# Attention with a layer norm and a gated feed-forward: the value products of the second pair of rows on stacked keys

## What is computed

```python
xn = layernorm(x)                                  # x: (8, 1024, 256)
q = (xn @ Wq + bq) in 8 heads of 128, + pe         # keys and values are shared by the heads
k, v = split(xn @ Wkv + bkv);  k = k + pe          # 128 columns each
probs = softmax(causal(q @ k.T / sqrt(128)))
attn = (probs @ v) @ Wo
out = x + attn + sigmoid(mr(xn) @ W_r.T) * (relu(mk(xn) @ W_k.T)**2 @ W_v.T)
```

## Time and profile before

| | |
|---|---|
| median of 3 runs | 1500.66 us (1500.39 to 1500.99) |
| the profiled execution, its own time | 1500.61 us |
| span of its instructions | 1498.9 us (1.7 us lie around it) |
| TensorE busy | 1477.3 us, 99% |
| VectorE, GpSimd, ScalarE busy | 1254.5 us (84%), 1158.2 us (77%), 1068.7 us (71%) |
| DMA | 171.73 MB, mean 115 GB/s |

### The profile page before, as it was taken

The page is one execution under the profiler, slowest core; times in us unless marked ns, Lnnn a source line. Parts: engine busy times, 40 slices in busy tenths (PEclk is TensorE's granted clock), DMA queues, the critical chain, the costliest instruction groups (busy, mean ns, idle before and its releaser), DMA issues.

```text
span 1498.9 us, 36110 instructions
## 1 busy us (share of the span) xinstructions
PE 1477.3 (99%) x11668; PEld 1443.2 (96%) x11668; DVE 1254.5 (84%) x3408; ACT 1068.7 (71%) x2547; POOL 1158.2 (77%) x1541
## 2 busy tenths in 40 slices
PE   7999999999999999999999999999999999999998
PEld 6999999999999999999999999999999999999998
DVE  6989868898688986889868898788977899778885
ACT  5777677776777767777677776777667776777774
POOL 5677877778777887777877778777787787877785
PEclk8999999999999999999999999999999999999999
DMA  4134532346214462144612346124551345502463
GB/s 130 33 107 131 181 95 56 109 132 192 75 52 125 133 186 75 50 123 135 192 60 67 117 143 188 46 75 119 162 173 34 85 125 157 173 25 85 127 182 128
DMA packets 225801, 171.73 MB, mean 115 GB/s; under 512 B 43600, under 2 KB 220880, under 8 KB 225616
## 3 DMA queue, kind: packets, MB, share of 16 engines
q1 hardware_dynamic: 224768, 169.03, 37.8%
q10 hardware_dynamic: 848, 0.40, 0.1%
HBM read 84.94 MB, written 81.26 MB: 111 GB/s over the span
## 4 chain that ended last, share of the span: by engine, by line
PE 85%; DVE 9%; issue 3%; POOL 1%; ACT 0%; DMA 0%; DVEq 0%; POOLq 0%; ACTq 0%
PE pS L1040 29%; PE pO L1181 22%; PE pG L1040 14%; PE pG L1127 9%; PE pT L1143 8%; DVE X L1019 2%; PE pS L1127 1%; DVE mix L860 1%; DVE Y L923 1%; DVE pt L943 1%; DVE xn L808 1%; POOL xt L509 1%; DVE ot L998 1%; DVE qtmp L849 1%; DVE kt L831 0%
## 5 line engine op out<-in xcount | busy, mean ns | idle before, releaser
L1040 PE MATMUL pS<-kt,qt 128*128 128x288 f32 (+41 forms) x2304 | 459.8, 329 | 1.7 <-POOL qt L521 1.1
L764 ACT ACTIVATE X<-X,bias 128x16 f32<-128x16 f32 (+56 forms) x512 | 375.9, 734 | 118.4 <-DVE bias L1019 117.7
L571 POOL TENSOR_SCALAR X<-X,rec 128x16 f32<-128x16 f32 (+56 forms) x512 | 379.2, 741 | 75.0 <-DVE rec L913 64.1
L1040 PEld LDWEIGHTS pS<-kt,qt 128*128 128x128 f32 x2304 | 366.1, 189 | 14.1 <-issue 2.0
L546 POOL TENSOR_TENSOR pt<-pt 128x896 fp32r<-128x896 f32 (+4 forms) x192 | 340.1, 1774 | 34.8 <-ACT pt L686 33.7
L1181 PE MATMUL pO<-pt,v 128*128 128x256 f32 x2192 | 307.1, 284 | 1.1 <-DVE ot L998 0.9
L1019 DVE CUSTOM_DVE_ANT_1 X<-pS,mask 128x528 f32<-128x528 f32 (+31 forms) x256 | 245.5, 959 | 37.8 <-PE pS L1040 33.4
L1181 PEld LDWEIGHTS pO<-pt,v 128*128 128x128 f32 x2192 | 272.0, 189 | 2.3 <-DVE ot L998 1.8
L757 ACT CAST ot<-pO 128x256 fp32r<-128x256 f32 x256 | 96.0, 375 | 203.0 <-PE pO L1181 116.9
L943 DVE TENSOR_TENSOR pt<-pt,pT 128x512 fp32r<-128x512 f32 (+3 forms) x424 | 197.3, 484 | 34.1 <-ACT pt L692 30.9
L692 ACT CAST pt<-pT 128x512 fp32r<-128x512 f32 (+3 forms) x432 | 182.0, 448 | 43.7 <-PE pT L1143 42.2
(11 more groups left out here) (123 smaller groups left out, 2259.3 us busy)
## 6 DMA issues: line engine op xcount, KB each, us to landing
park_dram<-Y SPq DMA_DIRECT2D x48, 448.0 KB, 3.2
pt<-park_dram SPq DMA_DIRECT2D x192, 112.0 KB, 3.0
park_dram<-Y SPq DMA_DIRECT2D x32, 512.0 KB, 2.9
pt<-park_dram SPq DMA_DIRECT2D x128, 128.0 KB, 2.9
park_dram<-Y SPq DMA_DIRECT2D x32, 384.0 KB, 2.9
pt<-park_dram SPq DMA_DIRECT2D x128, 96.0 KB, 2.4
park_dram<-Y SPq DMA_DIRECT2D x32, 320.0 KB, 2.7
pt<-park_dram SPq DMA_DIRECT2D x128, 80.0 KB, 2.2
```

What stands on the lines that cost most here:

```text
L571: nc.gpsimd.tensor_scalar(x_row(s, 0, w), x_row(s, 0, w), rec[:, j:j + 1], sign(s), ALU.mult, ALU.mult).then_inc(normed, 1)
L764: nc.scalar.activation(x_row(s, 0, w), x_row(s, 0, w), ACT.Exp, bias=bias[:, j:j + 1], scale=-1.0, accum_out=total[:, j:j + 1]).then_inc(e ...
L1040: last = nc.tensor.matmul(out, a[i], m[j], start=start and k == 0, stop=stop and k == n - 1)
```

## The change

The second pair of rows 1 to 7 (steps with `s % 8` of 2 and 3) has at most 64 keys in its diagonal block. Those keys are now written twice: on keys 0 to 63 and again on 64 to 127 of the block. Two tiles of values go with it: `vd` holds `v[0]` of the 64 keys on partitions 0 to 63 and `v[1]` on 64 to 127, `vz` holds `vn` on 0 to 63 and zeros below. `vd` x `pt[0]` and `vz` x `pt[1]` then take the place of the three products of that block. The other blocks of the pair keep three. Beside it `qtmp` has three slots in place of four, and some entries of the tables move. Of those in `F_LAG`, `H_LAG`, `L_LAG` and `W_LAG` only one concerns a step that is turned: the even steps of row 4 are fetched one iteration earlier.

```diff
-F_LAG = ((6, 1), (4, -2), (5, 4), (4, 3), (5, 3), (4, 1), (5, 5), (5, 2))
+F_LAG = ((5, 1), (4, -2), (5, 4), (4, 4), (4, 3), (4, 2), (5, 5), (5, 2))
-QTMP = 4
+QTMP = 3
-AT = {'stats': (-15, -8, -12, -7), 'apply': (-4, 0, 0, 0), 'inv': (-10, -5, -6, -3), 'mixr_prev': (0, 0, 0, 0), 'mixr_dve': (0, 0, 1, 0), 'mixr_out': (2, 1, 4, 1), 'ka_out': (4, 5, 9, 7), 'mixk_prev': (4, 7, 8, 4), 'mixk_dve': (6, 10, 8, 7), 'mixk_out': (9, 14, 11, 12)}
+AT = {'stats': (-15, -8, -14, -7), 'apply': (-4, -1, 0, 0), 'inv': (-12, -5, -6, -7), 'mixr_prev': (0, 0, 1, 0), 'mixr_dve': (0, 0, 1, 0), 'mixr_out': (2, 1, 4, 1), 'ka_out': (3, 4, 8, 7), 'mixk_prev': (4, 7, 8, 4), 'mixk_dve': (6, 10, 8, 9), 'mixk_out': (9, 14, 11, 12)}
...
+def doubled(s):
+
+    return s >= H and s % H // 2 == 1
...
+            def stack_two(b, c):
+
+                n = b * NC + c
+                sp.wait_ge(v_ready, n + 1)
+                if n:
+                    sp.wait_ge(pv_done, (n * TPC - 1) * PAIRS + 2)
+                tiles = slice(c * TPC, (c + 1) * TPC)
+                sp.wait_ge(v_neg, n + 1)
+                for to, part in ((vd[0:64, :, :], v[0]), (vd[64:P, :, :], v[1]), (vz[0:64, :, :], vn)):
+                    sp.dma_start(to.bitcast(F), part[0:64, tiles, :].bitcast(F)).then_inc(vd_loaded, 16)
+
             for b, it in turns():
                 if it < STEPS and it % PER == (2 if it >= PER else 11):
                     stack(b, it // PER)
+                if it < STEPS and it % PER == (6 if it >= PER else 13):
+                    stack_two(b, it // PER)
...
+                    elif doubled(s):
+                        own = (s % H + 1) * SUB
+                        last = x_row(s, s // H * P, (s // H + 1) * P).rearrange("p (i n) -> p i n", i=2)
+                        if own < 4 * SUB:
+                            nc.gpsimd.memset(last[:, :, own:4 * SUB], 0.0).then_inc(normed, 1)
+                        nc.gpsimd.tensor_scalar(last[:, 1, 0:own], last[:, 0, 0:own], rec[:, j:j + 1], sign(s),
+                                                ALU.mult, ALU.mult).then_inc(normed, 1)
+                        pool.wait_ge(normed, b * N_BODY + N_FIRST[s + 1] - 1)
...
+            nc.vector.memset(vz[64:P, :, :].bitcast(F), 0.0).then_inc(vs_zero, 1)
...
-                    work = [(k, i, j) for i, j in ((0, 0), (1, 0), (0, 1)) for k in range(plain)]
+                    work = ([(v[0][:, k, :], 0, k) for k in range(whole)] + [(v[1][:, k, :], 0, k) for k in range(whole)]
+                            + [(vd[:, tile, :], 0, k) for k in range(whole, plain)]
+                            + [(vn[:, k, :], 1, k) for k in range(whole)] + [(vz[:, tile, :], 1, k) for k in range(whole, plain)])
...
+                            if doubled(part):
+                                pe.wait_ge(vd_loaded, 48 * (b * NC + part // PER + 1))
```

More of the change, by code:

```diff
@@ L22 @@
 V_LAG = 3
[L23 to L26 removed]
+F_LAG = ((5, 1), (4, -2), (5, 4), (4, 4), (4, 3), (4, 2), (5, 5), (5, 2))
+H_LAG = ((6, 6), (6, 7), (7, 7), (7, 6), (7, 6), (7, 6), (7, 7), (7, 9))
+L_LAG = ((5, 4), (5, 5), (7, 6), (8, 12), (7, 9), (8, 13), (8, 7), (7, 7))
+W_LAG = ((9, 8), (11, 7), (8, 5), (6, 4), (7, 3), (7, 7), (8, 8), (8, 12))
 MODE = ('0000', '0000', '0111', '0111', '1111', '1111', '1313', '1111')
@@ L74, in packed, with used @@
     return s >= H and s % H < 2
+def doubled(s):
+    return s >= H and s % H // 2 == 1
+def used(s):
+    return 2 * SUB if packed(s) else 4 * SUB if doubled(s) else P
 def sign(s):
@@ L105, in scaled_by_act @@
 def scaled_by_act(s):
-    return s in SCALED and not packed(s)
+    return s in SCALED and not packed(s) and not doubled(s)
 def width(s):
@@ L178 @@
 T_BODY = T_FIRST[STEPS]
-N_FIRST = [sum((SUB * 2 if packed(r) else P) > (r % H + 1) * SUB for r in range(s))
-           + sum((not scaled_by_act(r)) + packed(r) for r in range(s)) for s in range(STEPS + 1)]
+N_FIRST = [sum(used(r) > (r % H + 1) * SUB for r in range(s))
+           + sum((not scaled_by_act(r)) + packed(r) + doubled(r) for r in range(s)) for s in range(STEPS + 1)]
 N_BODY = N_FIRST[STEPS]
@@ L222, in build @@
         vs = sb("vs", [P, TPC, D], R)
+        vd = sb("vd", [P, TPC, D], R)
+        vz = sb("vz", [P, TPC, D], R)
         vn = sb("vn", [P, NT, D], R)
@@ L292, in build @@
         vs_loaded = sem("vs_loaded")
+        vd_loaded = sem("vd_loaded")
         within_lo = sem("within_lo")
@@ L651, in v_out @@
                     act.wait_ge(vs_loaded, 48 * (chunk_no(b, c) - NC + 1))
+                    act.wait_ge(vd_loaded, 48 * (chunk_no(b, c) - NC + 1))
                 tiles = slice((c % NC) * TPC, (c % NC + 1) * TPC)
@@ L1156, in turn @@
                     plain = nk - packed(2 * pair)
+                    whole = nk - packed(2 * pair) - doubled(2 * pair)
+                    tile = part // H % TPC
                     summed = pO[:, 0:2 * P].rearrange("p (t a c) -> p t a c", t=2, a=4)
-                    work = [(k, i, j) for i, j in ((0, 0), (1, 0), (0, 1)) for k in range(plain)]
+                    work = ([(v[0][:, k, :], 0, k) for k in range(whole)] + [(v[1][:, k, :], 0, k) for k in range(whole)]
+                            + [(vd[:, tile, :], 0, k) for k in range(whole, plain)]
+                            + [(vn[:, k, :], 1, k) for k in range(whole)] + [(vz[:, tile, :], 1, k) for k in range(whole, plain)])
                     for n in range(len(work)) if part % 2 else ():
-                        k, i, j = work[n]
+                        standing, j, k = work[n]
                         if n == 0:
@@ L1171, in turn @@
                                     pe.wait_ge(t_hi, b * T_BODY + T_FIRST[s + 1])
-                        if n == 2 * plain:
+                        if n == len(work) - plain:
                             for s in (2 * pair + 1, 2 * pair):
@@ L1180, in turn @@
                                     pe.wait_ge(t_lo, b * T_BODY + T_FIRST[s + 1])
-                        last = nc.tensor.matmul(summed, (vn if j else v[i])[:, k, :],
-                                                pt_of(j, b, part)[:, :, :, k, :],
-                                                start=n == 0, stop=n == 3 * nk - 1)
+                        last = nc.tensor.matmul(summed, standing, pt_of(j, b, part)[:, :, :, k, :],
+                                                start=n == 0, stop=n == len(work) - 1 and not packed(part))
                     if part % 2:
@@ L1233, in _ @@
             pe.wait_ge(w_lo["wk"], 1)
-            pe.wait_ge(vs_zero, 1)
+            pe.wait_ge(vs_zero, 2)
             for b, it in turns():
```

2 lines of the change are left out of this document (1 added, 1 removed).

## The result

The changed kernel takes 1504.55 us (median of 8 runs, 1503.67 to 1505.42) against 1500.38 us (8 runs, 1499.62 to 1500.99): a ratio of 1.0026, 95% interval 1.0017 to 1.0035. The forecast was 1494.2 us with a range up to 1498.0.

The account below looks back on a forecast made before the run. TensorE was taken to bound the steady part; 1500.61 us less 6.5 us for 56 removed products, all else at nothing, gave 1494.1, forecast as 1494.2 us. The range was 1491.0 to 1498.0 us.

Parts of the forecast that it names:

- The bound: Steady part of the kernel: TensorE, busy 99% of the span, sets the time as long as the other engines keep up.
- The products: TensorE, second pairs of rows 1 to 7: 56 products less at 0.116 us each, 6.5 us off (6.3 to 7.8).
- third rival: Removed products only lengthen TensorE's wait for the same late tile, so nothing is gained: 1500.6 us, chance 0.05.
- Nothing for all of it: Query-sum slots, moved entries and the clear of vz cost zero, within -4.9 to +4 us.
- Slots and tables: Section on three query-sum slots and moved table entries: spare time suffices, no instruction is added or removed, cost nothing.
- the rival in which the tables cure TensorE's present waits: Moved entries also remove TensorE's existing waits: up to 4.9 us more gain, 1489.5 us, chance 0.08.
- I cost GpSimd's addition at nothing: GpSimd's added scalings, 43 us of its time (up to 80), stay hidden and add zero to the kernel's time.
- The margins: Room before TensorE needs late tiles: 2.35 us at the mask, 5.4 us at turned steps, against 0.45 to 0.78 us.
- The first rival: Lateness reaches TensorE at the start of rows 1 and 2 or at pO; 4 us return: 1498, chance 0.11.
- The port: GpSimd and two-SBUF-input VectorE work block each other: added scalings could take 0.68 us each, GpSimd 80 us in all.
- SyncE, slots, stacking waits: SyncE's 96 added transfers nearly all hidden (nothing to 43 us); three slots and the wait for vd_loaded cost nothing.
- What would show it: Profile signs: 56 matmuls less, GpSimd about 43 us busier; vd waits or TensorE waits over 8 us would refute.

Follow-up runs that it names:

- stack_bare: Changed kernel with the old tables, without GpSimd's second key copy and with the stacking transfers made for the first batch element only: 1496.49 us, ratio 0.9970.
- stack_no_copy: Changed kernel with the old tables and all transfers, without GpSimd's second copy of the keys (old clear in its place): 1496.59 us, ratio 0.9969.
- three_slots_only: Kernel before with three slots for the query sums in place of four, nothing else changed: 1500.82 us, ratio 0.9996.
- ka_only: Kernel before with one moved entry, ka_out (GpSimd's low part of ka) an iteration earlier in three chunks: 1508.60 us, ratio 1.0052.
- after_ka_inv_old: Changed kernel with the entries ka_out and inv as in the kernel before: 1497.21 us, ratio 0.9976.
- tables_only: Kernel before with all the moved table entries, without stacking (three products, four slots): 1505.86 us, ratio 1.0030.
- stack_old_tables: Changed kernel with the six tables of the kernel before (stacked pair, three slots): 1499.72 us, ratio 0.9988.

## Why the prediction was wrong

**The bound: right. The products: too large by about 2 us.** TensorE bounds the kernel before and after. In the traces a pair saves 0.11 to 0.12 us between the scores around it where nothing else moves (iterations 18, 26 and 34 of each batch element), as the distances in the earlier trace rows said. In the time, the products alone are worth 4.5 to 4.7 us (stack_bare, stack_no_copy; 3.3 by the traces), not 6.5, and the intervals end at 6.0 and 6.3. This term was too large, for the reason of my third rival ("TensorE waits for the same late tile anyway", chance 0.05): not at all pairs, but around iterations 34 and 50 TensorE next waits for `xt` or `ot`, and the saved time only lengthens the wait. These pieces are there with the copy and without, with the transfers and without, and not in three_slots_only. Of the waits in the earlier trace rows, one was for `xt`; I took it for something that the tables might cure, not for something that swallows a saving.

**"Nothing for all of it": this is the step that failed.** Under "Slots and tables" I costed the moved entries at zero with +4 us as the upper end, on the ground that they add no instruction, and looked at one of them (`mix` on ScalarE) for its wait. The one that counts, `ka_out`, I did not place beside VectorE's program at all. It puts a GpSimd operation of 1.3 us with two SBUF inputs, and the next one behind it, next to VectorE's two for `mix`, and costs 7.5 to 7.8 us (ka_only; after_ka_inv_old against the changed kernel). The other entries gain 2 to 4 us, near the rival in which the tables cure TensorE's present waits: the 2.6 us for `ot` did go (iteration 56 of each batch element is 0.69 us shorter with the new tables, of which 0.24 come back at 58). So the tables cost 4.5 us in sum (tables_only), beyond the +4 that I had as the upper end, and that upper end was not carried into the range: 1494.2 and 4 are 1498.2.

**"I cost GpSimd's addition at nothing": wrong by 3 to 4 us.** The added operations were sized about right: 414 and 321 ns on the chip (below), with 0.35 and 0.37 us forecast. GpSimd's busy time rose by 22.9 us and not by 43: 11 of the 43 were gaps of 0.10 us, which are not busy time, and the main scalings took 8.1 us less. The margins that I took from the timeline were those of row 3, and one example each. They hold there (iterations 26 to 29 are unchanged with the copy), but not everywhere: with the copy, iterations 31 and 32 are 0.2 us longer, and 63 another 0.12. A margin of 2.35 us read at one step said nothing of the steps at which VectorE's `kt` or the query sums come due. At iteration 63 (of the fourth batch element) VectorE and GpSimd are, in stack_old_tables with the copy:

```profile
748.73 0.99 DVE L866 SCALAR_TENSOR_TENSOR kt<-kv,kt 128x256 fp32r<-128x256 f32 x1
...
748.10 1.33 POOL L553 TENSOR_TENSOR qt<-qtmp,qt 128x512 fp32r<-128x512 f32 x1
```

and in stack_no_copy, without it:

```profile
745.43 0.42 DVE L860 SCALAR_TENSOR_TENSOR kt<-kv,kt 128x256 fp32r<-128x256 f32 x1 [0.61 <-ACT kt L673]
...
744.25 1.29 POOL L553 TENSOR_TENSOR qt<-qtmp,qt 128x512 fp32r<-128x512 f32 x1
```

The later scaling of `X` has pushed the pair together, `kt` takes 0.76 to 1.00 us in place of 0.42, and the first scores of the next batch element, which need it, start 0.12 us later. With the copy on ScalarE `kt` takes 0.43 to 0.45 again and those scores are on time. At iteration 31 no operation is stretched: the query sums on VectorE come 0.37 us later after the scores, and the next scores, which need them, 0.14. So the copy costs by plain lateness and by the port, at different places. The first rival (4 us given back, "where iterations are shortest") had the size, but not the place.

The added scalings in the changed kernel (GpSimd by line and shape):

```profile
L599 POOL TENSOR_SCALAR X<-X,rec 128x48 f32<-128x48 f32 x56 | 23.2, 414 | 0.0
...
L599 POOL TENSOR_SCALAR X<-X,rec 128x64 f32<-128x64 f32 x56 | 18.0, 321 | 0.0
...
L598 POOL MEMSET X<- 128x32 f32 x56 | 7.0, 125 | 4.6 <-DVE rec L949 3.5
```

**The port.** I had the mechanism in hand and read it one way. From a scaling of 0.97 us where 0.64 was normal I worked out how VectorE lengthens GpSimd's work, and took GpSimd's load for the price. The trace bears that out: VectorE's `xtok<-gate,xtok`, with two SBUF inputs, runs from 448.52 to 449.33 us, and the scaling starts under it at 448.87. What decides is the other direction, VectorE held by GpSimd: 0.87 us became 3.33 (3.11 in ka_only). The Trainium skill says it for both sides (SBUF — State Buffer, section Who interferes with whom): a VectorE operation with two SBUF inputs and a GpSimd operation that reads SBUF exclude each other for the whole instruction. The traces here agree, with 1.61 and 1.79 us for operations of 0.48, each ending 0.3 us after one of GpSimd's. Which of two operations is held cannot be read from the starts alone: the first `mix` has its start 0.03 us ahead of GpSimd's.

**SyncE, slots, stacking waits: right.** 84 of the 96 transfers left out made no measurable difference (0.9969 with all, 0.9970 without), three slots none, and no wait for `vd` appears.

**What would show it.** I wrote that TensorE's waits over 8 us would show the forecast wrong. They fell to 4.2 us and the forecast was wrong all the same. The sign was on another engine: VectorE's busy time, for which I had forecast nothing, was up by 37.6 us. That sign points at the mechanism and does not give a price: after_ka_inv_old has VectorE busy for 24.7 us more than the kernel before and is 3.6 us faster than it. What counts is which stretched operation TensorE waits for.

Together, in time: products -4.7, copy +2.9 to +3.9, `ka_out` +7.8, the other entries -3.3 (taken as the difference to tables_only's 4.5), transfers and slots 0. That is +2.7 to +3.7, and +4.2 us was measured, which the intervals (some 1.5 us each) allow. By the traces it is -3.3, +1.6 to +2.1 and +5.8, where the changed kernel has +2.6: the effects overlap where they meet (iterations 42, 50 and 58) and do not add up exactly.

## What to carry to other kernels

A table entry that adds no instruction is not free: one cost 7.8 us here. So write down what each moved operation will stand next to on the neighbouring engine, above all GpSimd's operations beside VectorE's with two SBUF inputs. If VectorE's or GpSimd's busy time rises more than its work, look for the same operation at two durations. Before counting a removed product as gain, look at what TensorE waits for next behind it. In a kernel bound by TensorE, read the distance between starts at the same place of both traces, since the list of waits misses whatever the pipelined matmul ahead covers. And when small work has to go somewhere, try an engine that does not hold up the next one in the chain: here that was ScalarE, where the copies were free, and not GpSimd.

## What the runs showed of the hardware

- VectorE's operations with two SBUF inputs stretched from 0.48 us to 1.61 and 1.79 beside GpSimd's operations of 1.29 and 1.75 us; masks that read PSUM did not (0.83 and 0.84 us). GpSimd's own two kept their time (1.29 us, and 1.75 beside 1.87 in the kernel before), but the next one, which started while VectorE's second still ran, took 1.49 in place of 1.29.
- A TensorE stall of 0.46 us was shown as 0.29 us idle, and in sum some 9 us of lost time (4.7 us of gain that did not arrive and 4.2 more) left the list of waits unchanged (4.9 and 4.2 us).
- A transfer of 64 partitions with 64 KB landed after 2.2 us, one of 32 partitions with 32 KB after 1.9, and 84 of the former more or less changed nothing.
- A value product whose stationary tile is half zeros (`vz`) took its 0.12 us like the others. 56 products less (0.11 to 0.12 us each, 6.5 us) brought 4.5 to 4.7 us.
